# Second attention: transposes moved next to the weighting matmuls, output projection moved half a group later

## The chip, the cores and the metric

One core of a Trainium2 chip runs the whole program. The metric is device time in microseconds of one execution; the kernel before was timed three times: 2059.51, 2060.38 and 2063.23 us, median 2060.38 us.

## The reference, cut to what matters

Two layers, each `x = x + attention(layernorm(x)) * silu(ffn(layernorm(x)))`, on x of 8 x 512 x 256. Only the second attention is touched:

```python
q, k, v = (xn @ w.T + b for w, b in ((wq, bq), (wk, bk), (wv, bv)))     # 8 x 512 x 256
q, k, v = (z.reshape(B, S, 16, 16).transpose(0, 2, 1, 3) for z in (q, k, v))
attn = softmax(q @ k^T / sqrt(16))                                      # 16 heads of width 16
out = (attn @ v).transpose(0, 2, 1, 3).reshape(B, S, 256)
s = out @ wo.T + bo
```

## The kernel before, in words

The program runs layer 0, then the experts of layer 1, then `attention1`, in that order; the change is in `attention1` alone. All numbers are float32, and matmuls take them as sums of a rounded part (hi) and the rest (lo).

`attention1` loops over 8 batches b, each with 4 groups g of 4 heads; q = 4b + g counts groups. Every engine has its own program for a group, written out by hand, with four **quarters** h = 0..3 (one per head) of four steps i = 0..3 (row tiles of 128). Engines meet through counting semaphores only, and each engine takes its instructions in the order of its program.

On TensorE (PE), each step (h, i) issues a *score* (`score`, L1382, into the two-buffer tile `ps`, for a head one group ahead) and a *transposed score* (`score_t`, L1390, into the two-buffer tile `pst`, for the present group). Since both tiles have two buffers, the score of a step waits until VectorE (DVE) has reduced the score two steps back (`maximum`, L1519, the row maximum `nm`), and the transposed score waits until ScalarE (ACT) has taken the exponential of the one two steps back (`exps`, L1626). At the end of every quarter comes a *weighting* of one key tile (`weigh`, L1400, eight matmuls in the trace, into `po`).

Between these steps PE issues other work:

- four *turns* of q and k (`turn_z`, L1374, four transposes each) for group q+2, into the two banks of the tile `w`, named `w1a` in the trace. ACT reads them out (`take_stack`: L1645 for j = 0, 1; L1649 for j = 2..5).
- one turn of the maxima (`turn_n`, L1410) at (3, 1) and one of the unnormalised output (`turn_o`, L1417) at (1, 2), both into the tile `pn`. DVE reads them out: `take_n` (L1533, two copies), `take_o` (L1539 reciprocal, L1541 product into `on`).
- in g = 1, the projection of the next batch (`project`, L1361 to L1363, four row tiles) through `w`.
- in g = 1, quarter 3, the two turns of the normalised output (`turn_on`, L1424). ACT rounds them (`ot_hi`, L1663), and DVE takes the rest (`split_ot`, L1553, two operations).
- in g = 2, quarter 3, the output projection of the batch before (`out_project`, L1434 to L1436), one row tile per step. DVE adds the bias (`take_out`, L1558) into the two-buffer tile `so`.

ACT rounds q and k of group q+3 at the head of quarter 3 (`split_z`, L1635 and L1638), GpSimd (POOL) takes the rests (its own `split_z`, L1314 and L1318). After POOL's `split_z` of g = 2, and in the same queue, comes `finish` (L1327 times the gate, L1329 plus x), four tiles of 128 rows. `take_out` of tile i waits until `finish` of tile i-2 is through, because `so` has two buffers and the semaphore `x_done` starts at 2.

Of the kernel before, what the change touches and what calls it, by code (L numbers as in the profile page):

```python
# [24 lines left out]
P = 128  # L25
B, T, C = 8, 512, 256
# [1138 lines left out]
def attention1(nc, c, io):  # L1165
# [12 lines left out]
    with ExitStack() as ctx:  # L1178
# [24 lines left out]
        on = t.sb("on", [P, NT, C])  # L1203
# [48 lines left out]

        TURNS = ((0, 0), (0, 1), (0, 3), (1, 1))
        STACKS = ((0, 0), (0, 1), (0, 3), (1, 0), (1, 1), (1, 2))
        PROJECTIONS = ((1, 3), (2, 0), (2, 2), (2, 3))

        with nc.Block() as block:
            @block.sync  # L1260
# [30 lines left out]
            def _(pool):  # L1291
# [39 lines left out]
                def row(b, first=False, last=False):  # L1331
                    for g in range(NG1):
                        if not (last and g > 0):
                            split_z(b + (g + 3) // NG1, (g + 3) % NG1)
                        if g == 2 and not first:
                            finish(b - 1)

                pool.sem_inc(x_done, 2)
# [7 lines left out]
            def _(pe):  # L1346
# [73 lines left out]
                def turn_on(b, k):  # L1420
                    if k == 0:
                        pe.wait_ge(on_done, NG1 * b + NG1)
                    for i in range(NT):
                        mm = pe.transpose(w[:, k, i * P:(i + 1) * P], on[:, i, k * P:(k + 1) * P], c.ident[:])  # L1424
                    mm.then_inc(on_turned, 1)

                def out_project(b, i):
# [10 lines left out]

                def group(b, g, first=False, last=False):
                    q = NG1 * b + g  # L1440
                    more1, more2 = (not (last and g + n >= NG1) for n in (1, 2))
                    back1, back2 = (not (first and g < n) for n in (1, 2))
                    projects = g == 1 and not last
                    for h in range(HG):
                        for i in range(NT):
                            if h < HG - 1 and more1:
                                score(q + 1, (g + 1) % NG1, h + 1, i)
                            elif h == HG - 1 and more2:
                                score(q + 2, (g + 2) % NG1, 0, i)
                            score_t(q, g, h, i)  # L1450
                            if (h, i) in TURNS and more2:
                                j = TURNS.index((h, i))
                                if j < 2 and g == 2 and not first:
                                    bank_read = (ot_lo_done, NC * b)
                                elif j < 2 and g == 3 and not first:
                                    bank_read = (so_done, NT * b)
                                else:
                                    bank_read = (stack_done, 6 * (q + 2) + (-2, 0, 1, 2)[j])
                                turn_z(q + 2, j, bank_read)
                            if (h, i) in PROJECTIONS and projects:  # L1460
                                if (h, i) == PROJECTIONS[0]:
                                    pe.wait_ge(xs_in, 32 * b + 64)
                                    pe.wait_ge(z_lo_done, 2 * q + 6)
                                project(b + 1, PROJECTIONS.index((h, i)))
                            if h == 1 and i == 2 and back2:
                                turn_o(q - 2, q + 1)
                            if h == HG - 1:
                                if i == 1 and more1:
                                    turn_n(q + 1)
                                if g == 1 and not first and i >= 2:  # L1470
                                    if last:
                                        pe.wait_ge(stack_done, 6 * (q + 2) + 3 + i)
                                    else:
                                        pe.wait_ge(qn_done, 2 * NT * (b + 1) + 5 + i)
                                    turn_on(b - 1, i - 2)
                                if g == 2 and not first:
                                    if i < 2 and not last:
                                        pe.wait_ge(stack_done, 6 * (q + 2) + 5 + i)
                                    out_project(b - 1, i)
                        if back1:  # L1480
                            weigh(q - 1, (g + 3) % NG1, h, b + 1 if g else b)

# [7 lines left out]
                for n in range(HG + 1):  # L1490
                    for i in range(NT):
                        score(n // HG, n // HG, n % HG, i)
                        if n < 2 and i % 2:
                            j = 2 * n + i // 2
                            turn_z(1, j, (stack_done, 6 + (-2, 0, 1, 2)[j]))
                pe.wait_ge(sel_copied, NG1)
                turn_n(0)
                for b in range(B):
# [15 lines left out]
            def _(dve):  # L1514
# [20 lines left out]
                def take_o(q, g):  # L1535

                    dve.wait_ge(o_turned, q + 1)
                    v = pn[:].rearrange("p (t h d) -> p t h d", t=NT, h=HG)
                    dve.reciprocal(inv[:], v[:, :, :, D1:D1 + 1]).then_inc(inv_done, 1)  # L1539
                    dve.wait_ge(inv_done, q + 1)  # L1540
                    dve.tensor_tensor(on[:, :, g * HG * D1:(g + 1) * HG * D1].rearrange("p t (h d) -> p t h d", h=HG),  # L1541
                                      v[:, :, :, 0:D1], inv[:].to_broadcast([P, NT, HG, D1]), ALU.mult).then_inc(on_done, 1)

                def take_proj(b, i):
# [15 lines left out]
                def group(b, g, first=False, last=False):  # L1560
# [4 lines left out]
                    for h in range(HG):  # L1565
                        if h == HG - 1 and more1:
                            split_n(q + 1, g + 1)
                        for i in range(NT):
# [4 lines left out]
                            if (h, i) in PROJECTIONS and projects:  # L1573
# [1 line left out]
                                    dve.wait_ge(vs_done, b + 1)  # L1575
                                    dve.wait_ge(z_lo_done, 2 * q + 6)
                                take_proj(b + 1, PROJECTIONS.index((h, i)))
                            if h == 1 and i == 3 and back2:
                                take_o(q - 2, (g + 2) % NG1)
                            if h == HG - 1:  # L1580
                                if i == 1 and more1:
                                    take_n(q + 1, (g + 1) % NG1)
                                if g == 1 and not first and i == 3:
                                    split_ot(b - 1)
                                if g == 2 and not first:
                                    take_out(b - 1, i)

                dve.memset(inv[:], 0.0).then_inc(max_done, 1)
                dve.wait_ge(sel_set, 5)
# [33 lines left out]
            def _(act):  # L1623
# [37 lines left out]
                def turn_on(b, k):  # L1661
                    act.wait_ge(on_turned, NC * b + k + 1)
                    act.copy(ot_hi[:, k, :], w[:, k, :]).then_inc(ot_hi_done, 1)  # L1663

                def group(b, g, first=False, last=False):
# [3 lines left out]
                    for h in range(HG):  # L1669
# [4 lines left out]
                        for i in range(NT):  # L1674
# [92 lines left out]
```

## Time and profile before

| | |
|---|---|
| median of 3 runs | 2060.38 us |
| profiled execution, its own time | 2060.63 us |
| its span, first to last instruction | 2058.9 us |
| second attention in the trace | about 1400 us to the end |
| PE busy, share of the span | 1896.0 us, 92% |
| DVE / ACT / POOL busy | 1444.2 / 1283.8 / 649.4 us |
| mean granted TensorE clock | 0.977 |

A line of waits names who waited for whom, in us in total, times, and the longest. A line of windows gives a stretch, its length, the busy time of PE, PE's weight loads, DVE, ACT and POOL (with counts), the granted TensorE clock (1.00 is 2.4 GHz, 0.50 is 1.2 GHz), and the DMA share. A line of the timeline gives start, duration, engine and line; where like instructions are merged (x2, x4), the duration is from the first start to the last end. Consecutive matmuls overlap in the trace: the distance between starts is what one costs.

### The profile page before, as it was taken

How to read it: one execution, taken by the hardware profiler on the slowest of the kernel's cores; microseconds unless marked ns; L12 is line 12 of the kernel's file. 1: busy time of each engine (PE TensorE's matmuls, PEld its weight loads, DVE VectorE, ACT ScalarE, POOL GpSimd, SP SyncE). 2: the span in 40 equal slices, each digit the busy share in tenths (PEclk: the TensorE clock that was granted, in tenths of full speed). 3: DMA queues.
4: the chain of work that ended last, by engine and by line, in shares of the span. 5: the costliest groups of instructions: out<-in, count | busy, mean ns of one | idle time of the engine just before them, and what ended most of it. 6: DMA issues, size and time to landing. Idle time of an engine off the chain costs nothing. (4 is left out here: it accounts for less than half of the span.)

```text
span 2058.9 us, 33528 instructions
## 1 busy us (share of the span) xinstructions
PE 1896.0 (92%) x12080; PEld 1468.2 (71%) x12080; DVE 1444.2 (70%) x2916; ACT 1283.8 (62%) x3061; POOL 649.4 (32%) x1021
## 2 busy tenths in 40 slices
PE   1999999999999999999999699975999999999997
PEld 1888878778878788888888588863656655655653
DVE  5786885977858858868678554425777777777773
ACT  3665674665756746657567564532677777777784
POOL 0353453543534535535435232222001011111112
PEclk9999999999999999999999899996999999999999
DMA  6110211111112111111111474302001011011001
GB/s 226 42 42 22 52 42 32 42 32 44 40 32 50 43 33 42 32 42 42 28 35 42 132 273 151 113 26 93 21 1 52 1 52 52 1 52 52 1 32 42
DMA packets 75748, 112.34 MB, mean 55 GB/s; under 512 B 8256, under 2 KB 49600, under 8 KB 75072
## 3 DMA queue, kind: packets, MB, share of 16 engines
q1 hardware_dynamic: 75040, 109.14, 18.1%
q8 instruction: 98, 1.61, 0.3%
q10 hardware_dynamic: 544, 1.05, 0.2%
q14 instruction: 66, 0.54, 0.1%
HBM read 55.64 MB, written 20.97 MB: 37 GB/s over the span
## 5 line engine op out<-in xcount | busy, mean ns | idle before, releaser
L1519 DVE TENSOR_REDUCE nm<-ps 128x1 f32<-128x512 f32 x512 | 336.8, 687 | 117.4 <-PE ps L1382 112.7
L1626 ACT ACTIVATE pt<-pst 128x512 f32<-128x512 f32 x512 | 296.9, 602 | 143.2 <-PE pst L1390 141.7
L804 POOL TENSOR_SCALAR pr<-pr,rinv 128x128 f32<-128x128 f32 (+3 forms) x512 | 264.1, 537 | 374.3 <-DVE rinv L692 374.3
L572 ACT ACTIVATE pr<-sc,nmax 128x128 f32<-128x128 f32 (+3 forms) x512 | 268.5, 527 | 143.4 <-DVE nmax L681 141.9
L681 DVE TENSOR_REDUCE nmax<-sc 128x1 f32<-128x128 f32 (+3 forms) x512 | 222.9, 483 | 76.7 <-PE sc L408 76.7
L1382 PE MATMUL ps<-kb,qb 96*128 96x512 f32 x512 | 238.9, 468 | 13.5 <-DVE nm L1519 11.1
L810 POOL TENSOR_TENSOR qk<-ra,rb 128x256 f32<-128x256 f32 x256 | 183.5, 739 | 206.6 <-DVE rb L703 170.8
L1390 PE MATMUL pst<-qb,kb 128*128 128x512 f32 x512 | 208.1, 408 | 6.7 <-ACT pt L1626 3.6
L1382 PEld LDWEIGHTS ps<-kb,qb 96*128 96x128 f32 x512 | 97.9, 192 | 145.4 <-issue 83.8
L420 PE MATMUL w<-ident,pr 128*128 128x128 f32 x1280 | 171.3, 281 | 25.7 <-DVE rb L703 19.8
L382 PE MATMUL w<-wq_hi,xt_hi 128*128 128x384 f32 x512 | 183.0, 358 | 2.4 <-DVE xt_lo L675 1.5
L404 PE MATMUL sc<-k,qs 128*128 128x256 f32 (+2 forms) x512 | 180.5, 363 | 3.0 <-DMA k<-k 2.9
L1314 POOL TENSOR_TENSOR zq<-qn,zq 128x256 fp32r<-128x256 f32 x32 | 23.8, 743 | 497.9 <-ACT zq L1635 497.9
L384 PE MATMUL w<-wq_hi,xt_lo 128*128 128x384 f32 x512 | 172.5, 337 | 0.0
L383 PE MATMUL w<-wq_lo,xt_hi 128*128 128x384 f32 x512 | 172.5, 337 | 0.0
L420 PEld LDWEIGHTS w<-ident,pr 128*128 128x128 f32 x1280 | 140.6, 143 | 42.7 <-DVE rb L703 29.2
L405 PE MATMUL sc<-k,qs 128*128 128x256 f32 (+2 forms) x512 | 163.0, 329 | 0.0
L432 PE MATMUL po<-pt,v_ring 128*64 128x512 f32 (+3 forms) x1024 | 151.9, 439 | 0.0
L1400 PE MATMUL po<-pt,vs 128*32 128x512 f32 x1024 | 135.7, 604 | 0.8 <-issue 0.8
L432 PEld LDWEIGHTS po<-pt,v_ring 128*64 128x64 f32 x1024 | 67.8, 136 | 82.9 <-issue 72.5
L1390 PEld LDWEIGHTS pst<-qb,kb 128*128 128x128 f32 x512 | 97.2, 191 | 31.5 <-ACT pt L1626 23.3
L701 DVE TENSOR_TENSOR ra<-w,rope 128x256 f32<-128x256 f32 x256 | 105.3, 411 | 17.1 <-ACT v_ring L582 10.2
(205 smaller groups left out, 4558.5 us busy)
## 6 DMA issues: line engine op xcount, KB each, us to landing
k<-k SPq DMA_DIRECT2D x256, 128.0 KB, 2.2
raw<-in_w SPq DMA_DIRECT2D x16, 640.0 KB, 5.7
raw<-in_w SPq DMA_DIRECT2D x8, 704.0 KB, 4.2
xa<-in_x SPq DMA_DIRECT2D x2, 2048.0 KB, 13.8
x<-in_x SPq DMA_DIRECT2D x8, 512.0 KB, 3.9
x_scratch<-x SPq DMA_DIRECT2D x8, 512.0 KB, 2.9
xt_hi_scratch<-xt_hi SPq DMA_DIRECT2D x1, 4096.0 KB, 14.0
xt_lo_scratch<-xt_lo SPq DMA_DIRECT2D x1, 4096.0 KB, 22.9
```

The costliest lines, as they stand in the source:

```text
L382: pe.matmul(w[:, bank, 0:PC0], xh, c.wq_hi[:, k, cols], start=(k == 0), stop=False)
L404: pe.matmul(out, q, k1[:, h, 0:width], start=(i != 1), stop=False)
L420: mm = pe.transpose(w[:, 1 - h + j, at:at + P], pr[:, h, SOFF[i] + kt * P:SOFF[i] + (kt + 1) * P], c.ident[:])
L432: mm = pe.matmul(po[h * D0:(h + 1) * D0, kt * P:T], v_ring[:, hp % 4 * NT + kt, h * D0:(h + 1) * D0], pt[:, h, PTOFF[kt]:PTOFF[kt] + T - k ...
L572: act.activation(pr[:, h, SOFF[i]:SOFF[i] + (i + 1) * P], sc[:, bank, at:at + (i + 1) * P], ACT.Exp, bias=nmax[:, h, i:i + 1], accum_out=r ...
L681: dve.tensor_reduce(nmax[:, h, i:i + 1], sc[:, bank, at:at + (i + 1) * P], AXX, ALU.max, negate=True).then_inc(max_done, 1)
L804: pool.tensor_scalar(p, p, rinv[:, h, i:i + 1], 1.0, ALU.mult, ALU.mult).then_inc(scaled, 1)
L810: pool.tensor_tensor(qk[:, i, :], ra[:, i % 2, :], rb[:, i % 2, :], ALU.add).then_inc(rope_done, 1)
L1382: pe.matmul(ps[:, i % 2, :], qb[0:2 * S3, g, h // 2, i * P:(i + 1) * P], kb[0:2 * S3, g, h, :], start=True, stop=True).then_inc(s_done, 1)
L1390: pe.matmul(pst[:, i % 2, :], kb[:, g, h, i * P:(i + 1) * P], qb[:, g, h // 2, :], start=True, stop=True).then_inc(st_done, 1)
L1519: dve.tensor_reduce(nm[:, g % 2, i, h:h + 1], ps[:, i % 2, :], AXX, ALU.max, negate=True).then_inc(max_done, 1)
L1626: act.activation(pt[:, g % 2, h, i, :], pst[:, i % 2, :], ACT.Exp).then_inc(exp_done, 1)
```

## The change

`on` gets a second copy, by the parity of the batch. The turns leave the inner steps and stand behind the four steps of a quarter, right before the weighting: turns 2 and 3 of group q+2 in quarter 0, `turn_o` in quarter 1, `turn_on` now in g = 2, quarter 2, and turns 0 and 1, now of group q+3, in quarter 3; two more turns stand ahead of the loop. `turn_n` stays at (3, 1). The projection of the next batch moves from (1, 3), (2, 0), (2, 2), (2, 3) to the four steps of quarter 2. The output projection and `take_out` move from g = 2, quarter 3 to g = 3, quarter 2; `finish` moves from g = 2 to g = 3, still behind POOL's `split_z`. On DVE, `take_o` moves from (1, 3) to (2, 0), and `split_ot` from g = 1, (3, 3) to g = 2, (3, 2). On ACT, `take_stack` runs at (0, 0), (0, 1), (1, 0) to (1, 3), and its `turn_on` moves to g = 2, (3, 0) and (3, 1).

```diff
-        TURNS = ((0, 0), (0, 1), (0, 3), (1, 1))
-        STACKS = ((0, 0), (0, 1), (0, 3), (1, 0), (1, 1), (1, 2))
-        PROJECTIONS = ((1, 3), (2, 0), (2, 2), (2, 3))
+        STACKS = ((0, 0), (0, 1), (1, 0), (1, 1), (1, 2), (1, 3))
+        PROJECTIONS = ((2, 0), (2, 1), (2, 2), (2, 3))
...
                         if not (last and g > 0):          # POOL
                             split_z(b + (g + 3) // NG1, (g + 3) % NG1)
-                        if g == 2 and not first:
+                        if g == 3 and not first:
                             finish(b - 1)
...
                             score_t(q, g, h, i)           # PE, inside the steps
-                            if (h, i) in TURNS and more2:
...
-                                turn_z(q + 2, j, bank_read)
...
-                            if h == 1 and i == 2 and back2:
-                                turn_o(q - 2, q + 1)
-                            if h == HG - 1:
-                                if i == 1 and more1:
-                                    turn_n(q + 1)
-                                if g == 1 and not first and i >= 2:
...
-                                    turn_on(b - 1, i - 2)
-                                if g == 2 and not first:
...
-                                    out_project(b - 1, i)
+                            if h == HG - 1 and i == 1 and more1:
+                                turn_n(q + 1)
+                            if h == 2 and g == 3 and not first:
+                                if i < 2 and more2:
+                                    pe.wait_ge(stack_done, 6 * (q + 2) + 4 + 2 * i)
+                                out_project(b - 1, i)
+
+                        if h == 0 and more2:              # behind the four steps
+                            for j in (2, 3):
+                                turn_z(q + 2, j, (stack_done, 6 * (q + 2) + j - 1))
+                        if h == 1 and back2:
+                            turn_o(q - 2, q + 1)
+                        if h == 2 and g == 2 and not first:
+                            for k in range(NC):
...
+                                turn_on(b - 1, k)
+                        if h == HG - 1 and more3:
+                            for j in range(2):
+                                if projects:
+                                    bank_read = (qn_done, 2 * NT * (b + 2))
+                                elif g == 2 and not first:
+                                    bank_read = (ot_lo_done, NC * b)
+                                elif g == 3 and not first:
+                                    bank_read = (so_done, NT * b)
+                                else:
+                                    bank_read = (stack_done, 6 * (q + 2) + 4 + 2 * j)
+                                turn_z(q + 3, j, bank_read)
                         if back1:
                             weigh(q - 1, (g + 3) % NG1, h, b + 1 if g else b)
...
+                for j in range(2):                        # ahead of the loop
+                    turn_z(2, j, (stack_done, 10 + 2 * j))
                 pe.wait_ge(sel_copied, NG1)
                 turn_n(0)
...
-                            if h == 1 and i == 3 and back2:   # DVE
+                            if h == 2 and i == 0 and back2:
                                 take_o(q - 2, (g + 2) % NG1)
+                            if h == 2 and g == 3 and not first:
+                                take_out(b - 1, i)
                             if h == HG - 1:
                                 if i == 1 and more1:
                                     take_n(q + 1, (g + 1) % NG1)
-                                if g == 1 and not first and i == 3:
+                                if g == 2 and not first and i == 2:
                                     split_ot(b - 1)
-                                if g == 2 and not first:
-                                    take_out(b - 1, i)
...
-                            if h == HG - 1 and g == 1 and not first and i >= 2:   # ACT
-                                turn_on(b - 1, i - 2)
+                            if h == HG - 1 and g == 2 and not first and i < 2:
+                                turn_on(b - 1, i)
```

## Rows read from the trace of the kernel before

**Rows 1.** Waits in the second attention: engine, line, waited for, total, times, longest
```profile
PEld ps L1382 <- DVE nm L1519: 49.7, 98, 1.3
DVE so L1558 <- POOL x_sb L1329: 3.3, 8, 1.4
```

**Rows 2.** Windows: g = 1 whole, then the quarters of g = 2 and of g = 3
```profile
1684.32:1708.82 24.50, 24.44 (x145) 17.21 (x145) 17.21 (x31) 15.14 (x30) 1.44 (x2) 1.00 0.00 1
1708.82:1714.24 5.42, 4.57 (x33) 2.74 (x29) 4.02 (x7) 4.18 (x8) 0.00 (x0) 1.00 0.01 3
1714.24:1718.19 3.95, 3.95 (x29) 2.43 (x25) 3.07 (x6) 3.18 (x7) 0.00 (x0) 1.00 0.00 0
1718.19:1721.73 3.54, 3.47 (x21) 1.46 (x17) 3.12 (x7) 3.15 (x8) 0.00 (x0) 1.00 0.00 0
1721.73:1728.06 6.33, 6.33 (x48) 4.87 (x45) 5.25 (x11) 3.21 (x7) 4.70 (x7) 1.00 0.00 0
1728.06:1732.81 4.75, 4.65 (x33) 2.75 (x29) 2.88 (x5) 3.98 (x8) 2.52 (x4) 1.00 0.24 81
1732.81:1736.77 3.96, 3.96 (x29) 2.44 (x25) 3.06 (x6) 3.29 (x8) 0.00 (x0) 1.00 0.20 44
1736.77:1740.30 3.53, 3.45 (x21) 1.45 (x17) 3.12 (x7) 3.16 (x8) 0.00 (x0) 1.00 0.95 299
1740.30:1744.50 4.20, 3.68 (x25) 1.94 (x21) 3.50 (x6) 3.07 (x8) 1.44 (x2) 1.00 0.66 247
```

**Rows 3.** Timeline of DVE in g = 3, quarters 1 to 3
```profile
1736.54 0.42 DVE L1541 TENSOR_TENSOR on<-pn,inv 128x256 f32<-128x256 f32 x1
1737.30 2.57 DVE L1519 TENSOR_REDUCE nm<-ps 128x1 f32<-128x512 f32 x4 [0.34 <-PE ps L1382]
1743.66 2.04 DVE L1519 TENSOR_REDUCE nm<-ps 128x1 f32<-128x512 f32 x3
```

**Rows 4.** Timeline of PE: an output projection, a turn before a weighting, a quarter's last step
```profile
1725.07 0.28 PE L1434 MATMUL w1a<-wo_hi,ot_hi 128*128 128x256 f32 x1
...
1725.78 0.40 PE L1382 MATMUL ps<-kb,qb 96*128 96x512 f32 x1
...
1731.28 0.60 PE L1374 MATMUL w1a<-ident,zk 128*96 128x128 f32 x4
...
1738.98 0.39 PE L1390 MATMUL pst<-qb,kb 128*128 128x512 f32 x1
```

**Rows 5.** Timeline of ACT in g = 3, quarter 1
```profile
1733.59 0.60 ACT L1626 ACTIVATE pt<-pst 128x512 f32<-128x512 f32 x1 [0.67 <-PE pst L1390]
1734.08 0.68 ACT L1649 ACTIVATE kb<-w1a,own 96x512 fp32r<-96x512 f32 x1
1734.65 0.59 ACT L1626 ACTIVATE pt<-pst 128x512 f32<-128x512 f32 x1
```

**Rows 6.** Timeline of all engines, around the handover from g = 1 to g = 2
```profile
1708.99 1.28 DVE L1553 TENSOR_TENSOR ot_lo<-w1a,ot_hi 128x512 fp32r<-128x512 f32 x2
...
1710.41 0.28 PE L1374 MATMUL w1a<-ident,zq 128*96 128x128 f32 x1 [0.85 <-DVE ot_lo L1553]
```

**Rows 7.** Timeline of all engines in g = 2, quarter 3: rounding, rests, finish, bias
```profile
1721.33 0.70 ACT L1635 CAST zq<-qn 128x256 fp32r<-128x256 f32 x2
...
1722.81 0.74 POOL L1318 TENSOR_TENSOR zk<-qn,zk 128x256 fp32r<-128x256 f32 x1
...
1723.71 0.73 POOL L1327 TENSOR_TENSOR so<-so,g_sb 128x256 f32<-128x256 f32 x1 [0.15 <-DVE so L1558]
...
1724.52 0.73 POOL L1329 TENSOR_TENSOR x_sb<-x_sb,so 128x256 f32<-128x256 f32 x1
...
1727.01 0.73 POOL L1329 TENSOR_TENSOR x_sb<-x_sb,so 128x256 f32<-128x256 f32 x1
...
1727.84 0.42 DVE L1558 TENSOR_TENSOR so<-w1a,bo_sb 128x256 f32<-128x256 f32 x1 [0.20 <-POOL x_sb L1329]
```

**Rows 8.** Windows at the end of the kernel, after the last weighting
```profile
2042.00:2048.00 6.00, 2.82 (x22) 2.01 (x19) 2.65 (x6) 1.66 (x3) 0.00 (x0) 1.00 0.01 3
2048.00:2051.00 3.00, 3.00 (x17) 3.00 (x16) 0.85 (x2) 0.00 (x0) 1.36 (x2) 0.52 0.00 0
```

More of the change, by code:

```diff
@@ L1202, in attention1 @@
         inv = t.sb("inv", [P, NT, HG, 1])
-        on = t.sb("on", [P, NT, C])
+        on = t.sb("on", [P, 2, NT, C])
         ot_hi, ot_lo = (t.sb(n, [P, NC, T], F32R) for n in ("ot_hi", "ot_lo"))
@@ L1423, in turn_on @@
                     for i in range(NT):
-                        mm = pe.transpose(w[:, k, i * P:(i + 1) * P], on[:, i, k * P:(k + 1) * P], c.ident[:])
+                        mm = pe.transpose(w[:, k, i * P:(i + 1) * P], on[:, b % 2, i, k * P:(k + 1) * P], c.ident[:])
                     mm.then_inc(on_turned, 1)
@@ L1440, in group @@
                     q = NG1 * b + g
-                    more1, more2 = (not (last and g + n >= NG1) for n in (1, 2))
+                    more1, more2, more3 = (not (last and g + n >= NG1) for n in (1, 2, 3))
                     back1, back2 = (not (first and g < n) for n in (1, 2))
@@ L1450, in group @@
                             score_t(q, g, h, i)
-                            if (h, i) in TURNS and more2:
[L1452 to L1458, printed above, removed]
-                                turn_z(q + 2, j, bank_read)
                             if (h, i) in PROJECTIONS and projects:
@@ L1464, in group @@
                                 project(b + 1, PROJECTIONS.index((h, i)))
-                            if h == 1 and i == 2 and back2:
-                                turn_o(q - 2, q + 1)
-                            if h == HG - 1:
-                                if i == 1 and more1:
-                                    turn_n(q + 1)
-                                if g == 1 and not first and i >= 2:
[L1471 to L1474, printed above, removed]
-                                    turn_on(b - 1, i - 2)
-                                if g == 2 and not first:
-                                    if i < 2 and not last:
-                                        pe.wait_ge(stack_done, 6 * (q + 2) + 5 + i)
-                                    out_project(b - 1, i)
+                            if h == HG - 1 and i == 1 and more1:
+                                turn_n(q + 1)
@@ new lines, in group @@
+                        if h == 2 and g == 2 and not first:
+                            for k in range(NC):
+                                if more2:
+                                    pe.wait_ge(stack_done, 6 * (q + 2) + 4 + 2 * k)
+                                turn_on(b - 1, k)
[10 more added lines that the diff above has]
+                                turn_z(q + 3, j, bank_read)
@@ L1540, in take_o @@
                     dve.wait_ge(inv_done, q + 1)
-                    dve.tensor_tensor(on[:, :, g * HG * D1:(g + 1) * HG * D1].rearrange("p t (h d) -> p t h d", h=HG),
+                    dve.tensor_tensor(on[:, q // NG1 % 2, :, g * HG * D1:(g + 1) * HG * D1].rearrange("p t (h d) -> p t h d", h=HG),
                                       v[:, :, :, 0:D1], inv[:].to_broadcast([P, NT, HG, D1]), ALU.mult).then_inc(on_done, 1)
```

## The prediction

> **What bounds the kernel now.** I read the windows of the second attention first, cut at the starts of the quarters, then the waits, then the timelines of single engines. PE is busy in 24.44 of the 24.50 us of g = 1 and in 3.45 to 6.33 us of nearly every other quarter [rows 2], so at first sight PE's own work sets the time. But busy time does not say how long a quarter must be. Quarter 2 of g = 3 has no turn in it and still takes 3.53 us, while quarter 1, with two turns more, takes 3.96 us [rows 2]: two turns cost 0.43 us together, not each. The reason is the handshake over two buffers. DVE reduces four scores in 2.57 us, 0.64 us each [rows 3], while PE issues a pair in about 0.47 us, so weight loads of scores wait 49.7 us for DVE [rows 1]. A turn inside the steps fills a wait that is there anyway. In quarter 0 the filler works for ACT's chain in the same way. That is the view in which the change must be costed: quarter by quarter, from the start of the first score to the last transposed score (T3 below), and from there to the next quarter.
>
> **The bricks.** From the start of T3 to the next quarter without a turn: 1740.30 - 1738.98 = 1.32 us. From a turn through the weighting to the next quarter: 1732.81 - 1731.28 = 1.53 us [rows 2, 4]. T3 to a turn behind it: 0.34 us where T3 itself had to wait, 0.24 us where not (estimates from the same steps: T3 of quarter 0 starts 2.88 us into it, the turn 3.22 us). A further turn behind the first: the row of four transposes spans 0.60 us of which the last is about 0.27, so 0.11 us a transpose and 0.44 us a turn; below it can hardly come under 0.36 us, above 0.49 us. So a turn next to a weighting has about the price of any turn, and none of the waits of the steps is filled by it.
>
> **The plain quarters (part 1 of the sum).** Starts are counted from the quarter's first score.
> - Quarter 0: T3 waits for the second exponential, which stands on ACT behind the copy of `po` and the first stack copy; both are still there. T3 stays at 2.88 us. Behind it now two turns: 2.88 + 0.34 + 0.44 + 1.53 = 5.19, against 4.75 us: +0.44.
> - Quarter 1: ACT now alternates exponential and stack copy four times. One pair takes 1734.65 - 1733.59 = 1.06 us [rows 5]; the first exponential starts at 0.78, the second ends at 0.78 + 1.06 + 0.60 = 2.44, T3 goes at 2.50. Then one turn: 2.50 + 0.34 + 1.53 = 4.37, against 3.96: +0.41. Its last stack copy ends 0.8 us into quarter 2 and delays nobody there.
> - Quarter 2: `take_o` leaves the shadow of a weighting and comes between the first and the second maximum, 0.25 us for the reciprocal (its first start to the next) and 0.42 us for the product [rows 3]. The second maximum then ends at 2.47 instead of 1.83, the last score waits for it, T3 goes at 2.87: 2.87 + 1.32 = 4.19, against 3.53: +0.66.
> - Quarter 3: T3 stays at 2.29. What went behind it was an idle 0.5 us in which PE waited for DVE after the weighting; that goes. 2.29 + 0.24 + 0.44 + 1.53 = 4.50, against 4.20: +0.30. Turn 0 of group q+3 now waits for POOL's rests, made in this same quarter: ACT's rounding starts 1.48 us before POOL's second operation, which takes 0.74 [rows 7]; it lands near 1.8 us, before the 2.5 us at which it is wanted. Covered, by 0.7 us.
> A plain group: +1.81 us on 16.44 [rows 2]. In g = 1, quarter 2 carries four projections and DVE has slack, so `take_o` is free there, and moving one projection over only moves it; its quarter 3 was 4.40 us with its two output turns and becomes 4.50. +0.48 +0.41 +0 +0.10 = +1.0 us.
>
> **g = 2 (part 2).** Quarter 0 was 5.42 us because the first turn waited 0.85 us for `split_ot` [rows 6]; that wait goes: 5.19, -0.23. Quarter 1: +0.42. Quarter 2 gets the two turns of the output: 2.87 + 0.24 + 0.44 + 1.53 = 5.08 against 3.54: +1.54. Quarter 3 loses the output projection but gets the wait back, larger. DVE starts the third maximum at 1743.66 - 1740.30 = 3.36 [rows 3], `split_ot` follows at 3.97 and takes 1.28, and PE goes 0.14 later [rows 6], at 5.39, with T3 long issued at about 2.4: PE stands idle for some 2.7 us. 5.39 + 0.44 + 1.53 = 7.36 against 6.33: +1.03. Together +2.8 us. If DVE's slack hid `split_ot`, it would be 2.7 us less; nothing in the order lets it.
>
> **g = 3 (part 3), the largest.** `take_out` of tile 2 waits for `finish` of tile 0. Before, `finish` stood behind POOL's `split_z` of the same quarter, and the wait was 3.3 us in 8 cases [rows 1]. Now `take_out` runs in quarter 2, while POOL is held in `split_z` of g = 3, which needs ACT's rounding at the head of quarter 3. In quarter 2, each output projection takes 1725.78 - 1725.07 = 0.71 us [rows 4]; DVE comes to `take_out` of tile 2 at 3.9 us. The last exponential of the quarter starts at 4.28, the rounding 0.49 later at 4.77, POOL's second rest 1.48 later at 6.25, the gate product 0.90 - 0.15 = 0.75 later at 7.00, the addition at 7.81, DVE's `take_out` 0.83 later at 8.64 [rows 7]. Behind it in DVE's queue stand the maximum of step 3 (8.99), `take_out` of tile 3, which needs the next POOL pair (1.5 us later, 10.14), `split_n` and the maxima of quarter 3. PE's second score of quarter 3 waits until 9.7, its last until 12.3, T3 12.64, then 0.24 + 0.44 + 1.53 = 14.85 us for quarters 2 and 3, against 3.53 + 4.20 = 7.73: +7.1. Without the stall it would be 5.95 + 4.50 = 10.45, so the stall alone is 4.4 us. With quarters 0 and 1: +8.0 us.
>
> **The clock.** At the end of the kernel PE has pauses, 2.82 us busy of 6, and then 3 us at a granted clock of 0.52, that is at 1.2 GHz for nearly all of it, with PE busy throughout [rows 8]. The stall in g = 3 leaves PE emptier than that for some 6 us. A low stretch of the same 3.5 us costs between 0 (PE waits for DVE anyway) and 1.75 us (all of it PE's work at half speed); I take 1.2, since turns and a weighting stand in it. The Trainium skill, "TensorE: Matmul & The Clock Gate", section "HAM oscillation — how this bites in real kernels", says that waits between bursts of matmuls drop the clock again each time they come. By that rule the term is there for every stall; without it, it is 0. The trace agrees in the end of the kernel.
>
> **The sum.** A batch: 1.8 + 1.0 + 2.8 + 8.0 = 13.6 us; six batches (b = 1 to 6) have all of it: 81. Batch 0 has no output work: 1 (its first group has no weightings, between 0 and 1.8) + 1.0 + 1.8 + 1.8 = 5.6. The two turns ahead of the loop replace two inside: 0. The last batch has no `split_z` ahead of `finish`, so no stall; its projection leaves a quarter and fills another whose T waits for ACT: between 0 and 8, taken 3.6. Clock 6 x 1.2 = 7. Sum 97.5 us, made against the profiled execution of 2060.6 us, which lies 0.3 us above the median shown: 2158 us.
>
> **The rivals.**
> - The stall is not there or is hidden (POOL gets to `finish` in time, or DVE catches up in the weighting): 6 x (4.4 + 1.2) less, 2158 - 34 = 2124. For it: before, only 3.3 us were lost at the same semaphore. Against: the order of POOL's queue. 0.17.
> - The clock falls deeper, so that the stall's low stretch reaches into the next group: 10 us of PE work at half speed, 5 us in place of 1.2, six times: 2158 + 23 = 2181. For it: nothing that says how long a low stretch lasts here. 0.12.
> - Only the two stalls of g = 2 and g = 3 count and the plain quarters cost nothing, because PE's work and not the handshake sets them: a batch loses 1.8 + 1.0 + 1.7 (g = 2, quarters 0 to 2) + 0.9 (g = 3, quarters 0 and 1) = 5.4 of its 13.6, the first and last batch 8: 97.5 - 32 - 8 leaves +57, 2118. Against: the 3.53 us of the empty quarter. 0.10.
> - Faster: a turn in the middle interrupts the scores; next to the weighting it would save about 0.08 us of the 0.44 (the 0.36 end above), 26 turns a batch, and the idle 0.5 us at the end of the groups and the 0.85 us go. 2.1 + 2.2 = 4.3 us in 8 batches: 2026. It decides only if PE is never short of reductions or exponentials while the turns stand outside the steps and POOL's order does not matter. 0.06. The change does nothing that is measured (the two cancel): 0.03.
> - My forecast: 0.52.
>
> What a measurement can tell from no change is 0.2%, 4 us. Faster 0.06, same 0.03, slower 0.91. The range takes in the first three rivals, widened by the bounds of the last batch and of a turn's price (six batches of 26 turns by 0.05 us is 8 us): 2110 to 2188.
>
> **What would show it.** In the profile after: DVE `so` waiting for POOL `x_sb` with some 5 us six times (about 30 us in all, from 3.3); PE's first turn of g = 2, quarter 3, waiting some 2.7 us for `ot_lo`; plain groups of about 18.2 us in place of 16.4, with the quarters at 5.2, 4.4, 4.2 and 4.5; DVE's product into `on` between the first two maxima of quarter 2; a granted clock under 1.00 once a batch. The prediction is wrong if plain groups stay at 16.4 us, or if POOL's `finish` starts before ACT's rounding of g = 3.

## The result

The changed kernel takes 2170.76 us (median of 4, 2169.03 to 2173.71) against 2061.59 us: ratio 1.0532, 95% interval 1.0513 to 1.0550. It is 109 us slower. Forecast were 2158 us, with a range of 2110 to 2188, and slower with a chance of 0.91. In the profiled executions, which are 108.4 us apart by their spans (2167.3 and 2058.9 us), a batch of the second attention takes 93.35 us on average (92.6 to 94.4) where it took 76.57 in each; six batches of that make 100.7 us of it. The six batches from g = 1 of b = 1 to g = 1 of b = 7, before and after:

```profile
1531.17:1990.59 459.42, 445.18 (x2593) 275.06 (x2593) 348.18 (x613) 337.64 (x667) 69.20 (x96) 1.00 0.10 33
1536.54:2096.64 560.10, 498.80 (x2596) 289.68 (x2593) 343.80 (x613) 338.36 (x666) 68.42 (x96) 0.95 0.08 27
```

The same windows as in [rows 2], of the kernel after: g = 1 whole, then the four quarters of g = 2 and of g = 3.

```profile
1723.50:1749.34 25.84, 24.88 (x141) 16.18 (x137) 16.92 (x31) 14.68 (x28) 1.44 (x2) 1.00 0.00 1
1749.34:1754.50 5.16, 4.58 (x28) 2.37 (x24) 2.73 (x5) 3.51 (x7) 0.00 (x0) 1.00 0.00 0
1754.50:1758.85 4.35, 4.18 (x24) 1.98 (x21) 2.58 (x4) 3.57 (x7) 0.00 (x0) 1.00 0.00 0
1758.85:1763.89 5.04, 4.45 (x28) 2.39 (x24) 3.52 (x8) 4.21 (x10) 0.49 (x1) 1.00 0.01 3
1763.89:1772.69 8.80, 6.31 (x33) 3.21 (x29) 5.14 (x8) 3.09 (x7) 0.95 (x2) 0.83 0.00 0
1772.69:1778.01 5.32, 4.75 (x28) 2.53 (x24) 2.58 (x4) 3.51 (x7) 0.00 (x0) 0.97 0.01 2
1778.01:1782.36 4.35, 4.18 (x25) 1.98 (x21) 2.57 (x4) 3.57 (x7) 0.00 (x0) 1.00 0.00 0
1782.36:1788.24 5.88, 5.88 (x44) 4.57 (x40) 3.14 (x7) 4.15 (x10) 0.32 (x1) 1.00 0.01 3
1788.24:1798.31 10.07, 6.50 (x32) 3.99 (x29) 5.67 (x11) 2.61 (x5) 6.79 (x10) 0.83 0.15 53
```

Read each against its partner in [rows 2]. PE's work over the six batches is the same (2593 and 2596 matmuls in the trace), and yet its busy time grows from 445 to 499 us: busy time is not a measure of the work here, and part of it runs at a lower clock. PE also waits more openly: in quarter 0 of g = 2, it is busy 4.58 of 5.16 us. Two quarters stand out: 8.80 us, where the first turn waits for `split_ot`, and 10.07 us, where DVE waits for POOL. Both have a granted clock of 0.83, where every line of [rows 2] has 1.00. This is one of the six batches; over all six, the first of the two takes 8.75 to 9.10 us and the second 9.83 to 10.89.

The stall, from the timeline of all engines in the kernel after (the answer to [rows 7]):

```profile
1787.15 0.70 ACT L1640 CAST zq<-qn 128x256 fp32r<-128x256 f32 x2
...
1788.62 0.73 POOL L1317 TENSOR_TENSOR zk<-qn,zk 128x256 fp32r<-128x256 f32 x1
...
1789.31 0.72 POOL L1326 TENSOR_TENSOR so<-so,g_sb 128x256 f32<-128x256 f32 x1
1790.11 0.72 POOL L1328 TENSOR_TENSOR x_sb<-x_sb,so 128x256 f32<-128x256 f32 x1
...
1790.94 0.42 DVE L1563 TENSOR_TENSOR so<-w1a,bo_sb 128x256 f32<-128x256 f32 x1 [4.87 <-POOL x_sb L1328]
1791.28 0.68 DVE L1524 TENSOR_REDUCE nm<-ps 128x1 f32<-128x512 f32 x1
...
1792.02 0.51 PE L1381 MATMUL ps<-kb,qb 96*128 96x512 f32 x1 [3.03 <-DVE nm L1524]
```

The chain is to be read downward: ACT's rounding lets POOL start, `finish` (the product and the sum) comes only behind it, DVE's bias addition has waited 4.87 us for it, the maximum behind it in DVE's queue comes late, and PE's score has waited 3.03 us for that maximum.

The waits of the second attention in the kernel after, which answer to [rows 1]:

```profile
PEld ps L1381 <- DVE nm L1524: 98.4, 181, 3.5
DVE so L1563 <- POOL x_sb L1328: 36.0, 16, 4.9
PE w1a L1373 <- DVE ot_lo L1558: 14.9, 6, 2.5
```

Two smaller readings. DVE in quarter 2 of a plain group, with `take_o` between the first maximum and the other three, where [rows 3] have four maxima in 2.57 us:

```profile
1715.39 0.69 DVE L1524 TENSOR_REDUCE nm<-ps 128x1 f32<-128x512 f32 x1 [1.77 <-PE ps L1381]
1716.00 0.25 DVE L1544 RECIPROCAL inv<-pn 128x16 f32<-128x16 f32 x1
1716.28 0.42 DVE L1546 TENSOR_TENSOR on<-pn,inv 128x256 f32<-128x256 f32 x1
1716.62 1.96 DVE L1524 TENSOR_REDUCE nm<-ps 128x1 f32<-128x512 f32 x3
```

And windows of the same batch, cut at PE's long pauses: the pause, and what the clock did behind it. The last three lines are from the batch before it, where the clock stayed low about twice as long behind each pause: g = 2, quarter 3, then quarter 0 of g = 3, into which the low stretch reaches, and quarter 3 of g = 3. Two of the six batches are like that, four like the first.

```profile
1766.70:1769.29 2.59, 0.10 (x2) 0.03 (x1) 2.56 (x5) 1.01 (x3) 0.00 (x0) 1.00 0.00 0
1769.29:1772.69 3.40, 3.40 (x17) 1.35 (x17) 0.45 (x1) 0.00 (x0) 0.00 (x0) 0.55 0.00 0
...
1788.59:1792.02 3.43, 0.40 (x3) 0.01 (x1) 1.02 (x2) 0.60 (x1) 3.27 (x6) 1.00 0.00 0
1792.02:1798.31 6.29, 5.74 (x26) 3.68 (x27) 4.65 (x9) 1.79 (x3) 3.16 (x5) 0.73 0.25 85
...
1669.44:1678.54 9.10, 6.61 (x32) 3.48 (x29) 5.14 (x8) 3.09 (x7) 0.94 (x2) 0.75 0.01 2
1678.54:1684.20 5.66, 5.25 (x28) 3.14 (x25) 2.67 (x4) 3.51 (x7) 0.00 (x0) 0.79 0.01 1
1694.44:1705.33 10.89, 7.80 (x32) 4.52 (x29) 5.67 (x11) 2.60 (x5) 6.76 (x10) 0.69 0.15 50
```

### The profile page after: what moved, and what is told of

The parts are those of the page before. It is cut to its first block and busy times, and to the rows that moved or that the text cites. A ratio compares the mean times of both kernels' runs of the same rounds, so it can differ in the third digit from the quotient of the medians.

```text
span 2167.3 us, 33527 instructions
## 1 busy us (share of the span) xinstructions
PE 1954.0 (90%) x12080; PEld 1480.7 (68%) x12080; DVE 1439.0 (66%) x2916; ACT 1283.6 (59%) x3061; POOL 649.0 (30%) x1021
## 3 DMA queue, kind: packets, MB, share of 16 engines
q10 hardware_dynamic: 544, 1.05, 0.1%
## 5 line engine op out<-in xcount | busy, mean ns | idle before, releaser
L1381 PE MATMUL ps<-kb,qb 96*128 96x512 f32 x512 | 246.2, 483 | 34.4 <-DVE nm L1524 28.3
L1389 PE MATMUL pst<-qb,kb 128*128 128x512 f32 x512 | 218.0, 427 | 22.7 <-ACT pt L1631 18.5
L1399 PE MATMUL po<-pt,vs 128*32 128x512 f32 x1024 | 141.0, 626 | 0.8 <-issue 0.8
```

Of the source, the lines that this page charges most:

```text
L1381: pe.matmul(ps[:, i % 2, :], qb[0:2 * S3, g, h // 2, i * P:(i + 1) * P], kb[0:2 * S3, g, h, :], start=True, stop=True).then_inc(s_done, 1)
L1389: pe.matmul(pst[:, i % 2, :], kb[:, g, h, i * P:(i + 1) * P], qb[:, g, h // 2, :], start=True, stop=True).then_inc(st_done, 1)
L1399: mm = pe.matmul(po[2 * D1 * h:2 * D1 * (h + 1), :], vs[:, kt, g * HG + h, :], pt[:, g % 2, h, kt, :], start=(kt == 0), stop=(kt == NT - 1))
```

## The experiments

All medians are of 4 or more executions, each compared with runs of the kernel before on the same chip (its median was 2059.8 to 2061.7 us).

**1. POOL's order.** In the changed kernel:

```diff
+                        if g == 3 and not first:
+                            finish(b - 1)
                         if not (last and g > 0):
                             split_z(b + (g + 3) // NG1, (g + 3) % NG1)
-                        if g == 3 and not first:
-                            finish(b - 1)
```

> The changed kernel with finish ahead of split_z in POOL's program of g = 3, nothing else. Stall theory: DVE's bias addition of tile 2 no longer waits for a POOL that is held in split_z. Quarters 2 and 3 of g = 3 fall from 15.9 to about 10.4 us; but POOL's rests now come behind four tiles of finish and end near 9.8 us, so the first turn behind the steps waits 1.4 us. Net 4.1 us less in six batches: 2170.8 - 25 = 2146 us; the 36 us of DVE so waiting for POOL x_sb fall under 8. Rival (DVE's and PE's load in these quarters, not POOL's order, makes them long): within 4 us of 2171.

Measured: 2144.11 us, ratio 1.0402 (1.0386 to 1.0417), where the changed kernel has 1.0532. Quarters 2 and 3 of g = 3 in this kernel:

```profile
1773.79:1779.68 5.89, 5.89 (x44) 4.57 (x40) 4.62 (x11) 4.15 (x10) 3.47 (x5) 1.00 0.01 3
1779.68:1785.59 5.91, 4.67 (x33) 2.73 (x29) 4.28 (x8) 2.47 (x5) 3.68 (x6) 1.00 0.27 90
```

11.80 us in place of 15.95, the clock at 1.00, and the wait for POOL down to 7.1 us. The order of two calls in POOL's queue costs 27 us of the 109. That is net: quarter 3 of g = 3 is still 5.91 us where it would be 4.49, because the first turn now waits for POOL's rests, which come behind `finish` (1.4 us a batch).

**2. `take_o` back at (1, 3)**, in the changed kernel:

```diff
-                            if h == 2 and i == 0 and back2:
+                            if h == 1 and i == 3 and back2:
                                 take_o(q - 2, (g + 2) % NG1)
```

> The changed kernel with DVE's take_o back behind the maximum of (1, 3), where the weighting covers it. Placement theory: quarter 2 of the plain groups falls from 4.2 to 3.53 us, in g = 0 and g = 2 of most batches (16 or 17 quarters of 0.66 us): 2170.8 - 11 = 2160 us. Quarter 2 of g = 3 is set by PE and stays. Rival (the longer quarter 2 comes from ACT's stack copies, late from quarter 1): no change, 2171; a second rival (DVE waits for turn_o and is late for the first maximum): slower, 2175 or more.

Measured: 2157.93 us, 1.0467 (1.0449 to 1.0484). Quarter 2 of the plain group is 3.55 us again, that of g = 2 4.41 in place of 5.04, that of g = 3 unchanged at 5.90. Placement theory, term by term; both rivals fall. One more thing stands in this trace. In one of its six batches the clock did not fall behind the pause in g = 2, quarter 3, and that quarter took:

```profile
1671.39:1678.76 7.37, 4.87 (x32) 2.80 (x28) 5.14 (x8) 3.09 (x7) 0.94 (x2) 1.00 0.01 2
```

**3. The output half alone.** On the kernel before: `on` double, `turn_on`, `split_ot`, output projection, `take_out` and `finish` where the change puts them; turns inside the steps as before. Its edit of the turns' bank waits:

```diff
-                                if j < 2 and g == 2 and not first:
+                                if j < 2 and g == 3 and not first:
                                     bank_read = (ot_lo_done, NC * b)
-                                elif j < 2 and g == 3 and not first:
-                                    bank_read = (so_done, NT * b)
+                                elif j < 2 and g == 0 and b > 1:
+                                    bank_read = (so_done, NT * (b - 1))
```

> The output half of the change alone: on double, turn_on in g = 2, output projection, take_out and finish in g = 3, split_ot in g = 2; turns, stack copies, projections and take_o stay inside the steps as before. Handshake theory: the stall of g = 3 is there (+6.2 us a batch in quarters 2 and 3), some 1.2 us of low clock behind it, and small terms of both signs cancel: +6.4 us in six batches, 2061.6 + 38 = 2100 us. Rival A (all of the loss is the output half): 2150 or more. Rival B (the turns carry all of it): within 4 us of 2062.

Measured: 2094.52 us, 1.0163 (1.0148 to 1.0178). The wait for POOL is 35.0 us, as in the changed kernel; quarters 2 and 3 of g = 3 take 5.88 + 9.14 us in this batch, and quarter 3 between 8.96 and 9.68 over the six. That is near the theory (2100 us) and far from both rivals.

**4. The turns' half alone.** On the kernel before: turns behind the steps, with stack copies, projections and `take_o`; the output work where it was.

```diff
+                        if h == 0 and more2:
+                            for j in (2, 3):
+                                turn_z(q + 2, j, (stack_done, 6 * (q + 2) + j - 1))
+                        if h == 1 and back2:
+                            turn_o(q - 2, q + 1)
+                        if h == HG - 1 and more3:
+                            for j in range(2):
...
+                                turn_z(q + 3, j, bank_read)
```

> The turns' half alone: turns behind the steps of a quarter, stack copies, projections and take_o moved with them; output projection, turn_on, split_ot and finish where they were before. Handshake theory: plain groups 18.2 in place of 16.4 us; in g = 1 the first turn of quarter 3 waits for split_ot (+3.5 us), in g = 2 it waits for the last bias addition (+2.2 us); 11.3 us a batch and up to 1.4 us for the clock: 2061.6 + 81 = 2143 us, and no DVE so wait above 1.5 us. Rival (turns next to a weighting cost less than in the middle, and PE's work sets the quarters): 2050 to 2065.

Measured: 2143.71 us, 1.0399 (1.0384 to 1.0415). Plain quarters are 5.18, 4.35, 4.17 and 4.49 us, the same as in the changed kernel. Quarter 3 of g = 1 in two batches, then of g = 2:

```profile
1644.32:1652.29 7.97, 5.45 (x40) 3.70 (x36) 5.14 (x8) 3.94 (x9) 1.44 (x2) 1.00 0.00 0
1732.32:1741.81 9.49, 6.95 (x41) 4.39 (x37) 5.14 (x8) 3.93 (x9) 1.44 (x2) 0.82 0.00 0
1755.50:1764.14 8.64, 7.37 (x56) 5.69 (x52) 5.46 (x10) 3.21 (x7) 6.86 (x10) 1.00 0.00 0
```

The turns' half gives the time that the handshake theory forecast. The two halves add to 5.6%, the whole change has 5.3%, but this is not a proof that they are separate: the turns alone pay 3.6 to 5.1 us a batch in g = 1, quarter 3, and 2.3 us in g = 2, quarter 3, for waits that the whole change has in other places and sizes. What the two have in common, the plain quarters, is alike to 0.01 us.

**5. The clock.** In the changed kernel, the two turns of g = 2, quarter 3, behind the weighting:

```diff
+                        if h == HG - 1 and g == 2 and not first and back1:
+                            weigh(q - 1, (g + 3) % NG1, h, b + 1)
                         if h == HG - 1 and more3:
...
-                        if back1:
+                        if back1 and not (h == HG - 1 and g == 2 and not first):
                             weigh(q - 1, (g + 3) % NG1, h, b + 1 if g else b)
```

> The changed kernel, but in g = 2, quarter 3, turns 0 and 1 stand behind the weighting instead of ahead of it. They wait for split_ot either way; now the weighting (1.0 us and its start) is done meanwhile, and PE's longest idle falls from 2.5 to about 1.2 us. Theory: 1.3 us of waiting less a batch, and the drop of the clock there (turns 1.60 and weighting 1.94 us long instead of 1.03 and 1.06, 1.4 us a batch) goes with the idle: six times 2.5, 2170.8 - 15 = 2156 us. Rival (the drop does not depend on that idle, or the clock drops later instead): only the waiting goes, 2163. Rival 2 (split_ot is late for another reason and takes the turns along): 2171.

Measured: 2159.00 us, 1.0468 (1.0452 to 1.0485), between the theory (2156) and its first rival (2163). First the stretch of g = 2, quarter 3, then quarter 3 of g = 3:

```profile
1762.00:1766.00 4.00, 2.46 (x20) 1.49 (x12) 3.13 (x6) 0.87 (x2) 0.00 (x0) 1.00 0.00 0
...
1784.00:1787.50 3.50, 2.94 (x10) 2.22 (x11) 3.07 (x7) 0.88 (x2) 3.08 (x5) 0.59 0.01 2
1787.50:1791.52 4.02, 4.02 (x18) 1.70 (x16) 1.58 (x3) 0.91 (x2) 0.00 (x0) 0.51 0.40 135
```

The drop at g = 2 is gone in all six batches: the quarter takes 6.20 us where it took 8.75 to 9.10, and the next one never more than 5.16. The drop at g = 3 is still there. The batch shown has the longest one of the six, 11.36 us; over all six, quarter 3 of g = 3 takes 9.43 to 11.36 us and 10.24 on average, against 10.25 in the changed kernel. So in the profiled execution the gain at g = 2 was real and nothing of it moved to g = 3: 15.7 us by the spans, as the theory has it. This execution (2153.3 us) was the fastest of the four, the others took 2158.5 to 2160.4. Why the median gains only 11.8 us is not shown; the mean granted clock of the others (0.968 to 0.970) is that of the profiled one (0.969).

**6. All three repairs** on the changed kernel (experiments 1, 2 and 5 together; the edits are those shown).

> The changed kernel with three repairs together: finish ahead of split_z on POOL (26.7 us alone), take_o back in the shadow of the weighting (12.8), turns of g = 2, quarter 3, behind the weighting (11.8). If the terms are separate they add: 2170.8 - 51 = 2119 us, and with no stall in g = 3 the low clock that moved there goes too, up to 8 us more: 2112 to 2120. The rest, about 55 us over the kernel before, would be the turns behind the steps. Rival (one cause stands behind all three): 2130 or more.

Measured: 2116.05 us, 1.0264 (1.0249 to 1.0279). The terms add to within 3.5 us (the three medians give 2119.5 us), and all six batches show a clock of 1.00 throughout. What is left over the kernel before, 54 us, has no output stall in it.

**7. Turns spread into the waits**, on the kernel before:

```diff
-        TURNS = ((0, 0), (0, 1), (0, 3), (1, 1))
-        STACKS = ((0, 0), (0, 1), (0, 3), (1, 0), (1, 1), (1, 2))
+        def turns(g, first):
+            return ((0, 0), (0, 1), (0, 2), (1, 1) if g == 1 else (2, 1))
+
+        def stacks(g, first):
+            return (((0, 0), (0, 1), (0, 3), (1, 0)) + (((1, 1), (1, 2)) if g == 1 else ((2, 1), (2, 2))))
...
-                            if h == 1 and i == 2 and back2:
+                            if (h, i) == (1, 2 if g == 1 else 1) and back2:
```

> The kernel before with the turns spread the other way, each into a step in which PE waits anyway: turn 2 from (0, 3) to (0, 2); where g is not 1, turn 3 from (1, 1) to (2, 1) with its stack copies at (2, 1) and (2, 2), and turn_o from (1, 2) to (1, 1). Handshake theory: quarter 0 4.75 to 4.38, quarter 1 3.96 to 3.5, quarter 2 stays at 3.53 though it has a turn more; 0.7 us a group, 2061 - 23 = 2038 us. Rival (PE's work sets the quarters, order does not matter): 2061. Rival 2 (ACT's later copies delay exponentials): 2065 or more.

Measured: 2055.05 us, 0.9969 (0.9960 to 0.9979). Faster, by a quarter of the forecast. Quarter 0 went to 4.40 as expected and quarter 2 stayed at 3.54 with a turn more in it, but quarter 1 stayed at 3.90. PE in quarter 1 of this kernel, last step:

```profile
1732.13 0.43 PE L1388 MATMUL ps<-kb,qb 96*128 96x512 f32 x1
1732.66 0.50 PE L1396 MATMUL pst<-qb,kb 128*128 128x512 f32 x1
```

The transposed score comes 0.53 us behind its score, 2.47 us into the quarter: it waits for ACT's exponential behind stack copy 3. The prediction had this 2.50 us in its own quarter 1, and I left it out here.

**8. `take_n` at (3, 2)**, on the kernel before:

```diff
-                                if i == 1 and more1:
+                                if i == 2 and more1:
                                     take_n(q + 1, (g + 1) % NG1)
```

> The kernel before with one move: DVE's take_n (two copies, 1.4 us) from (3, 1) to (3, 2), behind the third maximum of quarter 3. Theory: the 0.5 us at the end of plain groups is PE waiting for that third maximum, which stood behind take_n; it goes, and take_n still lands about when the first transposed score of the next group wants it: 0.45 us in some 24 groups, 2061 - 11 = 2050 us. Rival (the transposed score now waits for take_n as long as the score did for the maximum): 2061.

Measured: 2058.58 us, 0.9985 (0.9976 to 0.9995). Quarter 3 fell from 4.20 to 3.6 us, and the quarters 0 behind it rose from 4.7 to between 5.0 and 5.1: mostly the rival.

**9. Both together**, and the first three turns of g = 2 one step later (the `late` of experiment 12).

> Both edits on the kernel before, and in g = 2 turns 0 to 2 one step later, so that the first no longer waits 0.85 us for split_ot. If the terms add: 2061 - 23 - 11 - 5 = 2022 us. Rival (with PE shorter by 0.7 us a group DVE or ACT sets the quarters, and the edits do not add): 2030 to 2038.

Measured: 2053.18 us, 0.9958 (0.9943 to 0.9973). Neither was right: the terms do not add, as the rival says, but the gain is also far under the rival's 2030 to 2038. The quarters are 4.41, 3.91, 3.54 and 4.09; quarter 1 is where the missing gain sits.

**10. ACT's copies of k behind the steps of quarter 3**, stack copy 3 at (1, 3), POOL's `finish` ahead of `split_z` in g = 2, on top of experiment 9:

```diff
                         if h == HG - 1 and more3:
-                            split_z(b + (g + 3) // NG1, (g + 3) % NG1)
+                            split_z(b + (g + 3) // NG1, (g + 3) % NG1, (0,))
...
+                        if h == HG - 1 and more3:
+                            split_z(b + (g + 3) // NG1, (g + 3) % NG1, (1,))
```

> On top of the spread turns and the late take_n: ACT's copies are moved into the weighting's shadow too. Stack copy 3 goes from (1, 0) to (1, 3) where g is not 1, the two copies of k for group q+3 go from the head of quarter 3 behind its last exponential, and POOL takes finish ahead of split_z in g = 2. Traces of the two spread kernels show why they gained little: T3 of quarter 1 waited for ACT's exponential behind stack copy 3 (3.90 us where 3.5 was expected), and quarter 3 waited 0.3 us for the exponential behind the late copies. Theory: quarter 1 to 3.5, quarter 3 to 3.7, 0.8 us in some 22 groups: 2053 - 17 = 2036 us. Rival (ACT's copies then delay quarter 0, whose T3 is ACT's already): 2050 or more.

Measured: 2079.15 us, 1.0090 (1.0073 to 1.0107): slower. Quarters 1 to 3 reached 3.54, 3.54 and 3.62, but quarter 0 rose from 4.41 to 5.05 in g = 0, and in g = 3 from 4.57 to between 9.6 and 10.9. Its first turn waited 3.5 us there in each of six batches. The wait, that quarter in one batch, and POOL ahead of it:

```profile
PE w1a L1380 <- POOL zk L1324: 20.9, 6, 3.5
...
1731.65:1741.29 9.64, 6.16 (x32) 3.84 (x28) 3.31 (x6) 4.32 (x8) 3.97 (x6) 0.82 0.41 136
...
1733.69 0.72 POOL L1335 TENSOR_TENSOR x_sb<-x_sb,so 128x256 f32<-128x256 f32 x1
1734.37 0.72 POOL L1320 TENSOR_TENSOR zq<-qn,zq 128x256 fp32r<-128x256 f32 x1
1735.05 0.73 POOL L1324 TENSOR_TENSOR zk<-qn,zk 128x256 fp32r<-128x256 f32 x1
```

My mistake: what group q rounds is turned at the start of group q+1. I had counted a group of slack that isn't there. The trace puts most of the loss on the third of the edits: ACT's copies of k are done at 1731.26, and POOL comes to the rests only at 1734.37, behind `finish` of the last tile. The low clock follows behind the pause. Those quarters cost 5.7 us each more than in experiment 9, 34 us in all, while the time grew by 26. The edit that saved 27 us in g = 3 of the changed kernel (experiment 1) costs here, where the turns want the rests sooner. The late copies of k hold up the plain quarters 0: in g = 0 at 1751.98, they end at 1752.28, POOL's rest at 1753.09, and the turn starts at 1753.19. That is the delay of quarter 0 which the rival forecast, but by another way, since ACT's exponentials were not late. The three edits were not run one by one in this kernel, except stack copy 3, in experiment 11.

**11. Stack copy 3 alone** moved from (1, 0) to (1, 3) where g is not 1, on top of experiment 9.

> The spread turns with the late take_n (2053 us), and one more move: ACT's stack copy 3 from (1, 0) to (1, 3) where g is not 1. The rebalanced kernel reached 3.54 us in quarter 1 that way, and lost it in quarter 0, whose first turn waited for copies made too late; those stay early here. Theory: quarter 1 from 3.90 to 3.54, the others as they were: 0.36 us in 23 groups, 2053 - 8 = 2045 us. Rival (quarter 2 takes it back, since ACT's work only moves into it): 2053.

Measured: 2047.00 us, 0.9929 (0.9917 to 0.9941). Quarter 1 is 3.54 us, the others are unchanged: the theory, and the rival falls.

**12. `turn_o` in quarter 2 in place of turn 3.** The edits on the kernel before, beside those of experiment 8 and the use of the two functions:

```diff
+        def turns(g, first):
+            late = 1 if g == 2 and not first else 0
+            return ((0, late), (0, 1 + late), (0, 2 + late), (1, 1))
+
+        def stacks(g, first):
+            late = 1 if g == 2 and not first else 0
+            return (((0, late), (0, 1 + late), (0, 3)) + (((1, 0), (1, 1), (1, 2)) if g == 1 else ((1, 2), (1, 3), (2, 1))))
...
+                            if (h, i) == ((1, 2) if g == 1 else (2, 1)) and back2:    # turn_o
...
+                            if (h, i) == ((1, 3) if g == 1 else (2, 2)) and back2:    # take_o
```

> As the one with stack copy 3 moved, but turn 3 stays at (1, 1) and turn_o moves to (2, 1) instead, with DVE's take_o at (2, 2) and ACT's stack copies 3 to 5 at (1, 2), (1, 3) and (2, 1), where g is not 1: the last copies leave the end of quarter 2, so that the rounding of q and k at the head of quarter 3 is not late. Theory: quarters 4.4, 3.54, 3.54, 3.75: 0.7 us a group under the 2053 us kernel, 2037 us. Rival (ACT's copies at the end of quarter 1 delay quarter 2, or take_o delays the maxima of quarter 3): 2045 to 2053.

Measured: 2038.76 us, 0.9903 (0.9887 to 0.9919): 1% faster than the kernel before, and the fastest here. Four plain quarters, the last of g = 3 and then quarters 0 to 2 of g = 0:

```profile
1727.11:1730.74 3.63, 3.63 (x25) 2.00 (x21) 3.48 (x8) 3.22 (x8) 1.48 (x2) 1.00 0.83 301
1730.74:1735.40 4.66, 4.66 (x33) 2.69 (x29) 3.77 (x6) 3.65 (x8) 0.00 (x0) 1.00 0.00 0
1735.40:1738.93 3.53, 3.53 (x25) 1.88 (x21) 2.58 (x4) 2.89 (x6) 0.00 (x0) 1.00 0.00 0
1738.93:1742.46 3.53, 3.53 (x24) 1.90 (x20) 2.88 (x6) 3.53 (x8) 0.00 (x0) 1.00 0.00 0
```

Now one turn stands in each of quarters 1 and 2, at the 3.53 us that a quarter without a turn took before [rows 2]. Quarter 0 rose from 4.42 to 4.66, which the forecast (4.4) did not have, and quarter 3 fell to 3.63, below its 3.75.

## Why the prediction was right

- **Plain quarters.** Forecast 5.19, 4.37, 4.19 and 4.50; measured 5.18, 4.35, 4.17 and 4.49. The handshake over two buffers sets them, and a turn behind the steps costs its full price. Experiment 4 shows it by adding it and experiment 6 by leaving it in, experiments 7, 11 and 12 by turning it round: the same turns in other steps take less.
- **`take_o`.** Forecast 0.66 us in a quarter 2; experiment 2 gives 0.62 and 0.63.
- **The stall.** DVE waited 4.87 us, forecast "some 5". Quarters 2 and 3 of g = 3 were to be 14.85, plus the clock; they are 15.95 in the batch shown, 16.15 on average. The chain came as it was written down: ACT's rounding 4.79 us into quarter 2 (forecast 4.77), DVE's `take_out` at 8.58 (8.64), PE's second score of quarter 3 at 9.66 (9.7). Experiment 1 takes the stall away with one edit. The rival in which it is hidden falls.
- **g = 2, quarter 3.** Forecast 7.36 with PE idle for 2.7 us; idle 2.49, but the quarter takes 8.75 to 9.10. The mechanism was right and the size off: the clock drops here too, and the turns and the weighting run at 1.2 GHz for most of 3.4 us. In the one batch of experiment 2 in which it did not drop, the quarter takes 7.37 us. The sum had the clock's term once a batch, 1.2 us; it comes twice, some 1.6 us here, 0.2 in the next quarter and 1.3 in g = 3, on average. The step that was mis-sized is the one that put the pause of 2.7 us into the sum without asking what it does to the clock. The sentence in which every stall has the term stands in the prediction, but the sum did not follow it. Its 3.5 us for a low stretch is not in its rows either, which show 3 us at 0.52 [rows 8].
- **g = 1, quarter 0.** Forecast 5.19, measured 5.54. ACT's copy of v (`pass_v`) stands at the head of this quarter and was left out of its chain. The copy takes 1.05 us in the kernel after and before. Before, this quarter took 4.71 us as the others did; in experiment 7, where the other quarters 0 went to 4.40, this one stayed at 4.68, so it seems to have had a floor of its own that the turns inside had covered; no experiment moved `pass_v` alone. 0.35 us, seven times.
- **The sum.** A batch was to cost 13.6 + 1.2 = 14.8 us more and costs 16.8: g = 0 +1.8 as forecast, g = 1 +1.4 for 1.0 (`pass_v`), g = 2 +4.2 for 2.8 (the clock), g = 3 +9.4 for 9.2. Six times 2.0 is the 12 us by which the forecast would fall short. The first and last batch and the start, forecast at 9, take 7.7 (108.4 - 100.7), which offsets 1.5 us of it. The rival of a clock that falls deeper, 2181, is about as near in its total. Its mechanism came in part: in two of six batches the low stretch was about twice as long. But the one that reached into the next group came from the pause in g = 2, not from the stall in g = 3, and it added 0.5 us there.
- **The faster rival** (a turn in the middle costs 0.08 us more than next to a weighting): two turns next to the weighting take 0.96 us up to it (from 1721.54 to 1722.50 in the timeline of the kernel after), 0.43 more than one, which takes 0.53 (from 1713.33 to 1713.86). In the middle of a quarter, where PE does not wait, a turn adds 0.36: in the kernel before, the next score starts 0.59 us behind the transposed score with a turn between them (1728.40 to 1728.99) and 0.23 without (1730.21 to 1730.44). The saving that this rival wanted goes the other way.

## What to carry to other kernels

Where two engines hand over through two buffers, a stretch of loop has a floor that busy times don't show: measure one without filler work, and place the filler inside the waits, not at the stretch's end. When a consumer is moved earlier, look at the queue of the engine that frees its buffer: here one call in the wrong order on the least loaded engine cost 27 us. Neither order is right by itself: the same swap in another group went with a loss of 34 us in the quarters behind it, where the turns wanted what the queue held back (experiment 10). And follow each moved step one hand-over further than its own wait: the misses of experiments 7 and 10 came from the next engine's queue (ACT's stack copy 3, POOL's `finish` ahead of the rests).

## What the runs showed of the hardware that was not expected

Behind the same pause of PE, about 2.5 us long, the clock fell in some batches and not in others. PE waited up to 2.5 us for `split_ot`, six times, in the kernel after (14.9 us in all) and in experiment 4 (15.2 us). The kernel after has a low clock behind each of the six, the kernel of experiment 4 behind two; in its other four batches the clock is 1.00 throughout (7.97 us with 1.00 and 9.49 us with 0.82, above). Experiment 2 has it behind five of six. The low stretch that follows comes in two lengths, one about twice the other, in the same loop of the same kernel. What decides between them is left open, and so a forecast of such a term can only be a range: for the pause in g = 2 it was 0 to 1.7 us in the quarter itself. It also means that a single batch says little: the 11.36 us of experiment 5 look like a drop that grew, and the mean over six batches did not move.
